# A graph layer's neighbour sums: gathering 24 and matching ten tiles per unit, and half sums of one-hots

## The reference

```
x = layernorm(x + L(x))
L(h): e     = relu(bn(edge_attr @ ee_w1 + b1)) @ ee_w2 + b2     # 16 -> 128 -> 128, per edge
      h     = h + segment_sum(e, dst)                           # sum over a node's edges
      neigh = segment_sum(h[src], dst)                          # sum over a node's neighbours
      z     = h + neigh
      z     = relu(bn(z @ mlp_w1 + b1));  z = relu(bn(z @ mlp_w2 + b2));  return z
```

## Time and profile before

| | us |
|---|---|
| median of 3 runs (lowest, highest) | 2504.16 (2502.22, 2506.07) |
| profiled execution | 2505.9 |
| its span, first to last instruction | 2504.1 |

### The profile page before, as it was taken

The page is one execution under the profiler, slowest core; times in us unless marked ns, Lnnn a source line. Parts: engine busy times, 40 slices in busy tenths (PEclk is TensorE's granted clock), DMA queues, the critical chain, the costliest instruction groups (busy, mean ns, idle before and its releaser), DMA issues. The chain is left out here.

```text
span 2504.1 us, 79124 instructions
## 1 busy us (share of the span) xinstructions
PE 2196.8 (88%) x29440; PEld 1667.0 (67%) x29440; DVE 1940.1 (77%) x3008; ACT 648.5 (26%) x1189; POOL 1588.8 (63%) x1586
## 2 busy tenths in 40 slices
PE   3699999999968989999989999989999989999873
PEld 3699999999935666666666666666666666666532
DVE  5788888888888777777777777777777777777578
ACT  0022222222162222222222222222222222222176
POOL 3044444444387777777777777777777777777604
PEclk6799999999988999999999999999999999999885
DMA  5433333333252111111111111111111111111105
GB/s 143 158 99 94 101 98 95 101 96 96 88 188 56 53 53 53 53 53 53 53 53 53 53 53 53 53 53 53 53 53 53 53 53 53 53 53 53 44 26 179
DMA packets 96880, 183.68 MB, mean 73 GB/s; under 512 B 44996, under 2 KB 46676, under 8 KB 96654
## 3 DMA queue, kind: packets, MB, share of 16 engines
q1 hardware_dynamic: 51969, 97.47, 13.1%
q0 software_dynamic: 41376, 84.82, 12.3%
q10 hardware_dynamic: 3506, 1.04, 0.3%
HBM read 170.40 MB, written 12.80 MB: 73 GB/s over the span
## 5 line engine op out<-in xcount | busy, mean ns | idle before, releaser
L774 POOL DMA_INDIRECT table<-h_scratch,idx x1288 | 1215.5, 944 | 397.3 <-issue 391.3
L894 DVE TENSOR_TENSOR table<-ps,keys 128x1000 bf16<-128x1000 f32 x736 | 829.5, 1190 | 0.0
L811 PE MATMUL ps<-table,counts 128*32 128x384 bf16 x18400 | 781.9, 326 | 31.4 <-DVE summed L917 26.6
L811 PEld LDWEIGHTS ps<-table,counts 128*32 128x32 bf16 x18400 | 537.9, 97 | 293.6 <-ACT counts L855 115.7
L855 ACT CAST counts<-ps 128x500 bf16<-128x500 f32 x736 | 370.7, 590 | 1245.1 <-PE ps L798 1245.1
L524 POOL TENSOR_TENSOR ea_parts<-table 128x512 fp32r<-128x512 f32 x208 | 265.3, 1276 | 355.8 <-PE ps L540 286.2
L822 PE MATMUL ps<-table 128*128 128x96 f32 x2586 | 330.1, 280 | 124.6 <-DMA table<-h_scratch,idx 124.6
L822 PEld LDWEIGHTS ps<-table 128*128 128x128 f32 x2586 | 303.6, 192 | 191.7 <-issue 148.1
L555 PE MATMUL ps<-table 128*128 128x96 f32 x3328 | 415.0, 278 | 0.0
L555 PEld LDWEIGHTS ps<-table 128*128 128x128 f32 x3328 | 389.2, 193 | 0.0
L798 PE MATMUL ps<-table,low_match 128*128 128x500 bf16 x1472 | 343.5, 375 | 20.3 <-DVE table L894 20.0
(11 more groups left out here) (146 smaller groups left out, 1210.3 us busy)
## 6 DMA issues: line engine op xcount, KB each, us to landing
table<-in_edges_t SPq DMA_DIRECT2D x416, 128.0 KB, 2.5
table<-h_scratch,idx POOLq DMA_INDIRECT x1293
table<-in_edges SPq DMA_DIRECT2D x26, 512.0 KB, 4.6
table<-in_x_t SPq DMA_DIRECT2D x48, 256.0 KB, 2.9
h_scratch<-table SPq DMA_DIRECT2D x24, 256.0 KB, 2.0
out<-table SPq DMA_DIRECT2D x24, 256.0 KB, 2.0
idx<-in_src_tiles SPq DMA_DIRECT2D x92, 7.0 KB
table<-in_dst_mixed SPq DMA_DIRECT2D x1, 837.0 KB
```

Source lines behind the costliest of these rows:

```text
L774: pool.indirect_dma_start(rows[:, u, t * D:(t + 1) * D], None, h_dram, bass.IndirectOffsetOnAxis(ap=idx[:, u // 2, k:k + 1], axis=0)).then ...
L811: mm = pe.matmul(ps[32 * q:32 * q + PITCH, QUARTERS_BANK, 0:SPLITS * D], counts[:, k, b, :], h_split[:, at:at + SPLITS * D], start=(j < 4) ...
L894: dve.tensor_tensor(match[:, k], ps[:, 0, 0:LIST_COLS].unsqueeze(1).broadcast_to([P, DENSE, LIST_COLS]), keys[:, u % 2, c, :].unsqueeze(2) ...
```

## The change

Neighbour stage: 48 units of 34 tiles (two halves of 12 gathered and 5 dense tiles) and 29 tiles left over, gathered in five groups. A unit's 24 gathered tiles form four groups of six with windows of 64 nodes (before 96). Its ten dense tiles have windows of 12 nodes and are matched in pairs: five lists of 20 blocks, five pairs each, 480 compared elements per pair. Each tile has its own list product of 240 columns; ACT copies a pair's counts into its 24 of 120 columns (padded to 128) of one of two count buffers; and a pack is one product over all 128 output columns, for ten tiles at once. The pack of one list is issued in five parts between the list products of the next. There is one sum of splits and one fold (times the identity) per unit, ten dense adds per unit behind a register load each, spread over two lists of the next unit, and for the last unit all behind the last window add.

Edge stage: POOL adds the one-hot's first four tiles to its last four, as bf16 (`halve`), and PE makes four count products instead of eight. POOL's order is split g+1, halve g. Setup, base subtraction and key preparation follow the new shapes.

```diff
-DENSE = 2
-NARROW = 20
+NEAR = 64
+NARROW = 12
-LIST = 25
+LIST = 20
-GATHER = 7
+GATHER = 6
+STREAMS = 4
+DENSE = 10
+PAIRS = DENSE // 2
+PACKS = LIST // PAIRS
-MIXED = 184
+MIXED = 48
-RING = 4
+RING = 3
...
+                    def halve(i, u):
+                        pool.wait_ge(onehot_done, i * BODY + u + 1)
+                        wait(pool, sums_done, i * BODY + (u - 1))
+                        pool.tensor_tensor(halves[:, u % 2], onehot[:, u % 2, 0:GROUP_TILES // 2],
+                                           onehot[:, u % 2, GROUP_TILES // 2:], ALU.add).then_inc(halved, 1)
...
-                        for t in range(GROUP_TILES):
-                            pe.matmul(ps[:, 4 + 2 * (u % 2), WINDOW:2 * WINDOW], ones_bf[:],
-                                      onehot[:, u % 2, t, :].bitcast(BF16)[:, 1:2 * WINDOW:2],
-                                      start=(t == 0), stop=(t == GROUP_TILES - 1))
+                        pe.wait_ge(halved, g + 1)
+                        for t in range(GROUP_TILES // 2):
+                            pe.matmul(ps[:, 4 + 2 * (u % 2), WINDOW:2 * WINDOW], ones_bf[:], halves[:, u % 2, t, :],
+                                      start=(t == 0), stop=(t == GROUP_TILES // 2 - 1))
...
+                    def gather(g, u, v, at, tiles=GATHER):
+                        wait(pool, sums_done, g - (STREAMS - 1))
+                        pool.sem_inc(gathering, 1)
+                        for t in range(tiles):
+                            pool.indirect_dma_start(near_rows[:, u, t * D:(t + 1) * D], None, h_dram,
+                                bass.IndirectOffsetOnAxis(ap=idx[:, v, at + t:at + t + 1], axis=0)
+                            ).then_inc(gathered[u], 16)
...
+                    def list_pair(s, v, c, k):
+                        p = c * PAIRS + k
+                        pe.wait_ge(matched, s * LISTED + p + 1)
+                        wait(pe, list_kept, bank_freed(s, p))
+                        for t in range(2):
+                            mm = pe.matmul(ps[:, LIST_BANKS[p % RING], t * LIST_COLS:(t + 1) * LIST_COLS],
+                                           low_match[:, v, 2 * k + t, :], match[:, k, t, :], start=True, stop=True)
+                        mm.then_inc(listed, 1)
...
+                        for b in range(k * PACKS, (k + 1) * PACKS):
                             j = c * LIST + b
-                            q, at = j % 4, j * SPLITS * D
-                            mm = pe.matmul(ps[32 * q:32 * q + PITCH, QUARTERS_BANK, 0:SPLITS * D], counts[:, k, b, :],
-                                           h_split[:, at:at + SPLITS * D], start=(j < 4), stop=(j >= BLOCKS - 4),
-                                           tile_position=(0, 32 * q))
+                            mm = pe.matmul(ps[:, PACK_BANKS[v], 0:SPLITS * D], counts[(v * LISTS + c) % 2][:, b, :],
+                                           h_split[:, j * SPLITS * D:(j + 1) * SPLITS * D],
+                                           start=(j == 0), stop=(j == BLOCKS - 1))
...
+                            for c in range(LISTS):                      # PE, unit s
+                                for k in range(PAIRS):
+                                    list_pair(s, v, c, k)
+                                    if c:
+                                        pack(s, v, c - 1, k)
+                                    elif not (first and v == 0):
+                                        pack(s - 1, 1 - v, LISTS - 1, k)
+                                if c < STREAMS:
+                                    sums(s * STREAMS + c, c, s)
+                                if c == 1 and not (first and v == 0):
+                                    fold(s - 1, 1 - v)
...
+                    def unit(s, v, first=False, last=False):            # DVE
+                        for c in range(LISTS):
+                            if c == 0 and not last:
+                                make_keys(s + 1, 1 - v)
+                            if c == 1 and not first:
+                                sum_splits(s - 1, 1 - v)
+                            if c:
+                                add_window(s * STREAMS + c - 1, c - 1, (s - 1) * DENSE + max(c - 2, 0) * PAIRS)
+                            if c < STREAMS - 1:
+                                make_onehot(s * STREAMS + c + 1, c + 1, tiles_at(s, c + 1))
+                            if c == STREAMS - 1:
+                                make_onehot((s + 1) * STREAMS, 0, tiles_at(s + 1, 0))
+                            for k in range(PAIRS):
+                                if c < LISTS - 1:
+                                    match_pair(s, v, c + 1, k)
+                                elif not last:
+                                    match_pair(s + 1, 1 - v, 0, k)
+                                if c == 0 and not last:
+                                    match_low(s + 1, 1 - v, k)
+                                if c in (2, 3) and not first:
+                                    add_dense(s - 1, 1 - v, (c - 2) * PAIRS + k, s * STREAMS + c)
...
+                    for t in range(DENSE):                              # DVE, end of the stage
+                        add_dense(MIXED - 1, 1, t, NEAR_GROUPS + REST_GROUPS)
```

More of the change, by code:

```diff
@@ L817, in sums @@
+                    def sums(g, u, s, tiles=GATHER):
                         wait(pe, added, g - 1)
-                        wait(pe, dense_added, g - 2)
                         pe.wait_ge(onehot_done, g + 1)
-                        pe.wait_ge(gathered[u], (g - u) * (4 * GATHER) + 16 * tiles)
+                        pe.wait_ge(gathered[u], s * (16 * GATHER) + 16 * tiles)
                         for t in range(tiles):
-                            mm = pe.matmul(ps[:, 4 + 2 * (u % 2), 0:WINDOW], rows[:, u, t * D:(t + 1) * D],
-                                           onehot[:, u % 2, t, :], start=(t == 0), stop=(t == tiles - 1))
@@ L832, in body, with fold @@
+                        mm.then_inc(sums_done, 1)
+                    def fold(s, v):
+                        pe.wait_ge(splits_summed, s + 1)
+                        pe.matmul(ps[:, PACK_BANKS[v], SPLITS * D:(SPLITS + 1) * D], quarters, ident[:],
+                                  start=True, stop=True).then_inc(folded, 1)
                     def body(i, first=False):
-                        for u in range(BODY):
-                            g = i * BODY + u
+                        for v in range(2):
+                            s = i * 2 + v
@@ L835, in body @@
                             for c in range(LISTS):
-                                list_of(g, u, c)
-                            for c in range(LISTS):
-                                pack(g, u, c)
-                            mm = sums(g, u)
-                            if not (first and u == 0):
-                                mm = fold_quarters(g - 1, u - 1)
-                            mm.then_inc(sums_done, 1)
+                                for k in range(PAIRS):
[4 more added lines that the diff above has]
+                                        pack(s - 1, 1 - v, LISTS - 1, k)
@@ new lines, in add_window, with add_dense @@
+                        here = table[:, 0, bass.ds(at, NEAR)]
+                        dve.tensor_tensor(here, here, ps[:, 4 + 2 * (u % 2), 0:NEAR], ALU.add).then_inc(added, 1)
+                    def add_dense(s, v, t, windows):
+                        at = dve.value_load(base_i[0:1, bass.ds(s * DENSE + (DENSE_AT - GROUPS + t), 1)], min_val=0, max_val=N)
+                        dve.wait_ge(folded, s + 1)
+                        dve.wait_ge(added, windows)
+                        wait(dve, dense_added, s * DENSE + t)
@@ L940, in _ @@
+                    def body(i, first=False, last=False):
+                        for v in range(2):
+                            unit(i * 2 + v, v, first and v == 0, last and v == 1)
+                    move_base(dve, GROUPS, DENSE_AT, NEAR)
+                    move_base(dve, DENSE_AT, BASES_KEPT, NARROW)
+                    make_onehot(0, 0, 0)
                     dve.wait_ge(src_in, 16)
```

396 lines of the change are left out of this document (202 added, 194 removed).

## The result

The changed kernel takes 2327.43 us (median of 4, 2326.82 to 2328.88), the kernel before 2504.02 on the same chip (4 runs, 2502.22 to 2506.07): a ratio of 0.9295 [0.9279, 0.9311], 7% faster, 177 us. The forecast was 2342 in a range of 2325 to 2440. The profiled spans are 2504.1 and 2324.8, 179.3 apart.

What follows compares the result with a forecast made beforehand. POOL's gather chain was taken to bound the neighbour stage, PE the edge stage. Terms -139.8, -31, +8.3 and +0.5 gave -162 from 2505.9, so 2343.9, 2342 us as a median; range 2325 to 2440.

Steps and rivals of the forecast that it cites:

- The bound: Neighbour stage: POOL's gather chain bounds it, PE close behind; 112 fewer gathers at 1.2485 us give -139.8 us.
- PE's unit: Neighbour stage: PE's work for 34 tiles sums to 26.9 us (26.0 to 27.6), under POOL's 29.96.
- the pack: Neighbour stage, PE: products of 384 columns over all 128 output columns come every 0.164 us, bounds 0.160 and 0.32.
- The gathered pass: Neighbour stage, PE: each of two passes per gathered tile takes 0.104 us at 64 columns, between 0.085 and 0.117.
- DVE's unit: Neighbour stage: DVE needs 26.3 us for 34 tiles, with 1.0 us per match with a dense add.
- The tail: End of the neighbour stage: ten dense adds behind the last window add, uncovered, cost +8.3 us (1.6 to 8.3).
- The edge stage: Four fewer count products save 0.18 us per group on PE; 0.15 is taken, -31 us over 207 groups.
- the setup: Before the edge stage: minima reduced over 2176 instead of 2304 elements and one small store more; no change in time.
- the forecast itself: Whole kernel: the main case, 2328 to 2360 us, given 62%.
- A: Neighbour stage: list and pack changes bring PE to 31.9 us per unit, +93 us, about 2435; 18%.
- C: Neighbour stage: exposed register loads bring DVE to 35.2 us per unit, +252 us, about 2594, slower than before; 7%.
- B: Edge stage: POOL's halves are as dear as its slow adds, so little, nothing or a loss: 2356, 2373 or 2398; 10%.

## Why the prediction was right, and where its sum was off

**The bound.** The reading of the earlier trace rows against the busy shares of the earlier trace rows carried the forecast. PE looked fuller than POOL, but the gathers were evenly spaced and PE waited for them; 112 gathers at 1.2485 gave -139.8, and -139.4 came.

**PE's unit.** 26.9 forecast, 27.04 measured in the run with fewer gathers, 0.26 of it a hole that the sum did not have. Of its parts, the pack was the one without a row: 0.164, taken from the list rows near the lower of its bounds (0.160 and 0.32). The pair of list products with four packs took 0.853 to 0.86 where 0.862 had been summed. The gathered pass was 0.108 for 0.104. A pack comes to (0.853 - 2 x 0.103) / 4 = 0.162 us. The Trainium skill (TensorE: Matmul & The Clock Gate, Back-to-back issue gap) gives 131 ns at N=512 as sustained; 384 columns took longer than that here, so the trace goes against it.

**DVE's unit.** The match with a dense add was undersized, 1.13 for 1.0, ten times per unit. It cost nothing, because DVE stayed under PE and PE under POOL: the run with a third fewer gathers passes a unit in 27.04 with DVE's adds all in it.

**The tail.** +8.3 forecast, +7.7 measured, and -8.8 when all ten adds are moved.

**The edge stage.** "I take 0.15 of the 0.18" gave -31; -34.3 came, 0.166 per group. The halves took 1.0 us for 0.96 and lay under PE. DVE's nearness, for which 0.03 had been taken off, cost nearly nothing.

**The step that failed** is the setup: "The mixed minima are reduced over 2176 instead of 2304 elements and lie in front of loads that come later; one small store more", at nothing. It is the term of the sum that was mis-sized: 0 forecast, -13.9 measured. Its words look at DVE's work and at what comes behind it. What set the reduction's start was the load ahead of it, 20.41 us of waiting in the trace of before, and the diff turned that load from 93 partitions to 99. The wait was there to be seen; the shape of the load behind it was not looked at. With 14 us more the sum would have been 2328, where 2327 was measured. Without them the measured time came out just below the band of the forecast itself (2328 to 2360) and 2 us inside the lower end of the range.

**The rivals.** A (PE takes over) and C (DVE takes over) fell with the run of fewer gathers, B (the edge stage gives little, nothing or loses) with the one of eight counts: 34.7 us are lost without the halves, where B has them bring 17 at the most. In B's terms the halves ran at 1.0 us on every one of 208 instances; the 1.60 of the node stage did not appear.

## What to carry to other kernels

When two engines look full, the spacing of the one's instructions and the other's wait row say which is the bound; then sum up the next engine's unit from spacings, not from bars, and take that margin as the room for the next step (here 2.9 us, which a unit of 30 tiles uses up: there PE is the bound). Measure a unit between the same event of two units, not as a mean over a whole stage with other work at its end. When a diff changes the shape of a load, look at the number of its partitions and not only at its bytes, and at who waits for it: padding 93 to 96 was worth 15 us without any other change. Adds behind a register load go where the engine waits anyway, and not at the end of a stage.

## What the runs showed of the hardware

- A load of 837 to 952 KB, issued from SP's queue at 3.3 to 3.5 us, was waited for until 32.86 us at 93 partitions, 18.89 at 96, 18.61 at 99, 36.95 at 106 and 19.28 at 112. The plateau in the throughput was 75 GB/s at 93 and 50 at 106, against 402 to 416 in the first slices.
- Products of 384 bf16 columns over all 128 output columns, four behind two of 240, repeat every 0.853 to 0.86 us, in the changed kernel (granted clock 0.98 over the stretch) and in the run with fewer gathers (1.00); at the first list of a unit it is 1.11 us.
- On DVE, a match of 480 elements followed by an add of 12 elements behind a register load repeats every 1.13 us, with 0.35 us of idle time ahead of the add. Dense adds alone repeat every 0.85 us, with 0.68 idle.
- POOL's add of 384 f32 elements into bf16 took 0.995 to 1.012 us on 208 instances in the edge stage, beside DVE operations that read PSUM.
